# GNN layer on one core: layer 3's weights copied to SBUF by ScalarE, and the order of VectorE's step changed

## The reference, cut to what matters

```
h = relu(layernorm(x))                      # 12500 nodes x 128
l1 = per-node linear of h                   # 128 values: 32 scalars, 3 x 32 vectors
rbf = cut(d) * sin(n*pi*d/6) / (n*pi*d/6)   # 8 values for each of 200000 edges
weight = silu(silu(rbf @ fc_w1) @ fc_w2) @ fc_w3     # scales left out; 4 x 32 per edge
w00, w01, w10, w11 = split(weight, 4)
gs, gv = l1[src]                            # gather by edge
o00 = w00 * gs * sh0
o01 = w01 * gs * sh1                        # 3 x 32
o10 = w10 * gv * sh0                        # 3 x 32
o11 = w11 * sum_m(gv * sh1) / sqrt(3)
agg = segment_sum([o00, o11, o01, o10], dst) / count
out = x + sc(h) + tanh(agg @ alpha_w) * (agg @ lin2)
```

## Time and profile before

| | us |
|---|---|
| median of 3 runs (lowest, highest) | 2507.67 (2504.34, 2520.52) |
| the profiled execution | 2501.21 |
| its span, from first to last instruction | 2499.4 |
| first gather starts, last gather starts | 69.3, 2470.5 |
| mean granted clock of PE, share of full speed | 0.829 |

### The profile page before, as it was taken

How to read it: one execution, slowest core, us unless ns; L and a number is a source line. 1 busy time by engine, 2 the same in 40 slices (tenths; PEclk the granted TensorE clock), 3 DMA queues, 4 the chain that set the end, 5 groups by cost and what they waited for, 6 DMA issues and landing times. The chain is left out here.

```text
span 2499.4 us, 33478 instructions
## 1 busy us (share of the span) xinstructions
PE 1807.8 (72%) x7969; PEld 1166.1 (47%) x7969; DVE 1770.3 (71%) x4669; ACT 1018.1 (41%) x3049; POOL 1529.5 (61%) x1624
## 2 busy tenths in 40 slices
PE   6467667776887777777677776677776777877777
PEld 5244445444554444444444444444544544544444
DVE  7576677667667767766676667767676766677677
ACT  6344444444444444333333333334443433334343
POOL 7466566666666666666666666666565656556563
PEclk9688888888877888778787878889888888889879
DMA  7322222222222222222222222223232222222232
GB/s 213 67 63 66 53 66 66 59 62 66 64 56 65 65 58 62 55 49 51 46 51 48 48 48 52 58 45 67 53 67 55 63 63 64 53 64 59 60 66 55
DMA packets 347698, 155.72 MB, mean 62 GB/s; under 512 B 237983, under 2 KB 322048, under 8 KB 347584
## 3 DMA queue, kind: packets, MB, share of 16 engines
q0 software_dynamic: 50016, 102.51, 15.7%
q1 hardware_dynamic: 296938, 51.75, 11.4%
q10 hardware_dynamic: 630, 0.29, 0.0%
HBM read 134.27 MB, written 20.15 MB: 62 GB/s over the span
## 5 line engine op out<-in xcount | busy, mean ns | idle before, releaser
L967 POOL DMA_INDIRECT lin_g<-lin_table,src_ix x1563 | 1480.4, 947 | 929.4 <-issue 454.5
L1154 ACT ACTIVATE lin_sh<-lin_g,harm 128x128 f32<-128x128 f32 x1563 | 484.0, 394 | 256.3 <-DMA lin_g<-lin_table,src_ix 249.7
L1398 DVE TENSOR_TENSOR msg<-lin_sh,ps_w 128x576 f32<-128x576 f32 (+1 forms) x261 | 196.0, 751 | 520.1 <-remote 293.3
L1037 PE MATMUL ps_sums<-near_sums,far_hot 128*128 128x257 f32 x520 | 207.7, 487 | 433.8 <-DVE agg L1457 165.0
L1015 PE MATMUL ps_w<-w,h 128*128 128x256 f32 x1566 | 473.7, 448 | 61.6 <-DVE msg L1403 50.9
L1027 PE MATMUL ps_near<-msg,onehot 128*64 128x257 f32 x3126 | 500.3, 465 | 0.0
L1015 PEld LDWEIGHTS ps_w<-w,h 128*128 128x128 f32 x1566 | 400.8, 275 | 179.2 <-DVE msg L1403 63.7
L1161 ACT ACTIVATE near_sums<-ps_near 128x257 f32<-128x257 f32 x261 | 100.5, 385 | 809.5 <-remote 519.2
L996 PE MATMUL ps_h<-rbf,w 32*128 32x192 f32 x1044 | 271.4, 384 | 155.8 <-DVE rbf L1352 75.3
L1027 PEld LDWEIGHTS ps_near<-msg,onehot 128*64 128x64 f32 x3126 | 239.1, 162 | 226.0 <-issue 172.7
L1037 PEld LDWEIGHTS ps_sums<-near_sums,far_hot 128*128 128x128 f32 x520 | 102.7, 228 | 501.9 <-issue 356.8
(11 more groups left out here) (174 smaller groups left out, 1556.5 us busy)
## 6 DMA issues: line engine op xcount, KB each, us to landing
lin_g<-lin_table,src_ix POOLq DMA_INDIRECT x1563
dist_in<-in_edge_weight SPq DMA_DIRECT2D x67, 96.0 KB
lin_table<-lin_out SPq DMA_DIRECT2D x24, 256.0 KB, 2.4
x_in<-in_x SPq DMA_DIRECT2D x24, 256.0 KB
skip_table<-x_in SPq DMA_DIRECT2D x24, 256.0 KB
xq<-in_x SPq DMA_DIRECT2D x23, 256.0 KB, 3.6
harm<-in_edge_attr SPq DMA_DIRECT2D x66, 48.0 KB
x_in<-skip_table SPq DMA_DIRECT2D x8, 256.0 KB
```

What stands on the lines that cost most here:

```text
L967: pool.indirect_dma_start(slot_tiles(s, u)[rows, t, :], None, lin_table, bass.IndirectOffsetOnAxis(ap=src_ix[rows, s.phase, u, col:col + 1 ...
L1037: pe.matmul(ps_nodes(i), far_hot[:, u, :], near_sums[:, u % 2, :], start=True, stop=True).then_inc(sums_ready, 1)
L1154: last = act.activation(lin_sh0[:, u % 2, j, :], slot_tiles(s, u)[:, j, :], ACT.Copy, scale=harm[:, s.phase, u, harm_col(j):harm_col(j) + 1])
L1398: dve.tensor_tensor(o10[:, h], scaled[:, h, MUL:].rearrange("p t (m c) -> p t m c", m=3), spread_m(w_part(2))[:, h], ALU.mult)
```

## The change

Three edits. `copy_w(g+1)`, new, on ACT between `silu2` and `scale_lin`: one activation of 768 columns from `ps_w` to `w_sb`, two buffers in SBUF that share the memory of `key_all` (used only before the first group). It waits for `w_ready` of its group and for `w_read` of the group two before. PE's `layer3` now waits for `w_copied` in place of `w_read`, and `late` waits for `w_copied` in place of `w_ready` and reads the weights from `w_sb`. On DVE `products(g+2)` and `columns(g+2)` now stand ahead of `late(g+1)`, for which `dot` has two buffers. Before the first group ACT waits until all keys are stored, and copies group 0's weights ahead of the first two `scale_lin`.

```diff
+            w_sb = key_all
-            dot = s2("dot", [P, TILES, MUL])
+            dot = s2("dot", [P, 2, TILES, MUL])
...
-            def w_part(i):
-
-                return ps_w[:, 0:TILES * P].rearrange("p (t w c) -> p t w c", t=TILES, c=MUL)[:, :, i, :]
+            def w_part(u, i):
+
+                return w_sb[:, u % 2, :].rearrange("p (t w c) -> p t w c", t=TILES, c=MUL)[:, :, i, :]
...
-                            at_least(pe, w_read, i * SLOTS + u)
+                            at_least(pe, w_copied, i * SLOTS + u)
...
+                        def copy_w(i, u):
+
+                            i, u = i + u // SLOTS, u % SLOTS
+                            n = i * SLOTS + u
+                            act.wait_ge(w_ready, n + 1)
+                            at_least(act, w_read, n - 1)
+                            act.activation(w_sb[:, u % 2, :], ps_w[:, 0:TILES * P], ACT.Copy).then_inc(w_copied, 1)
...
+                        for b in range(GB):
+                            act.wait_ge(key_out[b], 16)
+                        copy_w(0, 0)
                         for u in range(2):
                             scale_lin(turn_of(0), u)
...
                                     silu2(i, u + 2)
+                                copy_w(i, u + 1)
                                 if share and u == 0:
                                     center(i)
...
-                            dve.wait_ge(w_ready, n + 1)
+                            if last_group(i):
+                                dve.wait_ge(msg_ready, n)
+                            dve.wait_ge(w_copied, n + 1)
                             dve.wait_ge(lin_sh0_ready, n + 1)
...
+                                if not last or u < SLOTS - 1:
+                                    products(s, u + 2)
+                                    columns(s, u + 2)
                                 late(s, u + 1)
                                 if u == 2 and share:
                                     skip_sum(i)
                                 if u == 2 and not last:
                                     fractions(i + 2)
-                                if not last or u < SLOTS - 1:
-                                    products(s, u + 2)
-                                    columns(s, u + 2)
```

More of the change, by code:

```diff
@@ L644, in gnn_kernel @@
             key_all = s2("key_all", [P, 2, GROUP])
+            w_sb = key_all
+            assert GB == 3
             harm = s2("harm", [P, RING, SLOTS, 4 * TILES])
@@ L722, in gnn_kernel @@
             h1_done, h1_ready, h2_done, h2_ready = sem("h1_done"), sem("h1_ready"), sem("h2_done"), sem("h2_ready")
-            w_ready, w_read, msg_ready, sums_ready = sem("w_ready"), sem("w_read"), sem("msg_ready"), sem("sums_ready")
+            w_ready, w_copied, w_read = sem("w_ready"), sem("w_copied"), sem("w_read")
+            msg_ready, sums_ready = sem("msg_ready"), sem("sums_ready")
             onehot_ready, lin_sh_ready, dot_ready = sem("onehot_ready"), sem("lin_sh_ready"), sem("dot_ready")
@@ L1385, in columns @@
                             dve.wait_ge(lin_sh_ready, n + 1)
-                            dve.tensor_reduce(dot[:, h], lin_sh[:, h].rearrange("p t m c -> p t c m"), AX_X, ALU.add).then_inc(dot_ready, 1)
+                            dve.tensor_reduce(dot[:, u % 2, h], lin_sh[:, h].rearrange("p t m c -> p t c m"), AX_X, ALU.add).then_inc(dot_ready, 1)
                         def late(s, u):
@@ L1394, in late @@
                             scaled = lin_sh0[:, u % 2]
-                            dve.wait_ge(w_ready, n + 1)
+                            if last_group(i):
+                                dve.wait_ge(msg_ready, n)
+                            dve.wait_ge(w_copied, n + 1)
                             dve.wait_ge(lin_sh0_ready, n + 1)
                             at_least(dve, near_ready, n - 1)
-                            dve.tensor_tensor(o10[:, h], scaled[:, h, MUL:].rearrange("p t (m c) -> p t m c", m=3), spread_m(w_part(2))[:, h],
+                            dve.tensor_tensor(o10[:, h], scaled[:, h, MUL:].rearrange("p t (m c) -> p t m c", m=3), spread_m(w_part(u, 2))[:, h],
                                               ALU.mult)
-                            dve.tensor_tensor(o00[:, h], scaled[:, h, 0:MUL], w_part(0)[:, h], ALU.mult)
-                            dve.tensor_tensor(w_s[:, h], w_part(1)[:, h], lin_s(s, u)[:, h], ALU.mult).then_inc(w_s_ready, 1)
+                            dve.tensor_tensor(o00[:, h], scaled[:, h, 0:MUL], w_part(u, 0)[:, h], ALU.mult)
+                            dve.tensor_tensor(w_s[:, h], w_part(u, 1)[:, h], lin_s(s, u)[:, h], ALU.mult).then_inc(w_s_ready, 1)
                             dve.wait_ge(dot_ready, n + 1)
-                            dve.scalar_tensor_tensor(out=o11[:, h], in0=dot[:, h], scalar=float(3 ** -0.5), in1=w_part(3)[:, h],
+                            dve.scalar_tensor_tensor(out=o11[:, h], in0=dot[:, u % 2, h], scalar=float(3 ** -0.5), in1=w_part(u, 3)[:, h],
                                                      op0=ALU.mult, op1=ALU.mult).then_inc(w_read, 1)
```

## The result

The changed kernel takes 2485.53 us (median of 4 runs, 2480.2 to 2493.36) where the kernel before, run beside it, takes 2509.92 us. The ratio is 0.990, 95% interval 0.9866 to 0.9935: 1% faster. The profiled execution took 2485.61 us, its span 2483.8 us, at a mean granted clock of 0.826.

A forecast was written before the change was run, and what follows sets the result against it. POOL's program, its gathers plus 475 us of stops, was taken as the span. The profiled 2501.2 + 14 - 12 + 1 = 2504 us, with the median 6.5 us above, gave 2510, own range 2485 to 2532, 8 in 10 2440 to 2580.

The forecast's parts named there:

- The step that failed: POOL's program is the span; only its 475 us of stops, or the 1.25 us per gather, can move the time much.
- the move: DVE's products and columns put ahead of the message: VectorE's waits shrink beside POOL's stops; cost 0, no gain.
- The other half of the step: PE's semaphore updates are late during a long run of POOL gathers and come about 2.5 us after it ends.
- Operands from SBUF: Four instructions of late, now with both operands in SBUF, delay POOL's gathers: 14 us, ends 0 and 70.
- the quadratic bound of 0.27 us a group: Upper end for gathers beside late: every gather beginning inside a two-SBUF-operand product waits for the rest; 70 us in all.
- 6 ns for each L1436: Small price of a DVE instruction with two SBUF operands, from mean gather times of 0.943 to 0.945 against 0.946 us.
- rival 2: Slower by the port: VectorE's SBUF operands lengthen POOL's gathers, up to 70 us, 2566 us; chance 0.2.
- Layer 3 freed from o11: PE's layer 3 waits for the copy and no longer for o11: a gain of 12 us, ends 0 and 53.
- The copy: ACT's 768-column copy from PSUM, 0.80 us each: cost 0 under the new order, 104 us without that cover.
- Rival 3: Slower by ACT: it stops at the copy for layer 3's late update, delaying scale_lin and copy_near; 104 us, 2612; chance 0.1.
- The start: Group 0's copy and a scale_lin delay its message up to 2.7 us, layer 3 starts 0.8 earlier: 1 us cost.
- Rival 1: Faster: the new order gets PE's updates out before they are held and POOL's stops go; 78 us, 2432; chance 0.27.

The follow-up runs named there:

- the order alone: Kernel before with only VectorE's new order (products and columns ahead of the message), no copy: 0.9798, 0.9857 and 0.9901 of the kernel before.
- set 4: Changed kernel (0.9921), the order alone (0.9901), the copy alone (1.0238), and changed kernel with layer 3 also waiting for w_read (0.9927); kernel before 2512.91 us.
- set 2: Kernel before, changed kernel, the order alone, and changed kernel with layer 3 also waiting for w_read, on one chip: 0.9996, 0.9972, 0.9857, 1.0025 of 2218.14 us.
- set 1: The order alone, the copy alone and the unread copy, beside the kernel before (2561.44 us) on one chip: 0.9798, 1.0066, 0.9852.
- set 3: The order alone plus one unused VectorE product per group, second operand in SBUF (0.985) or PSUM (0.9884); also the unread copy (0.9921) and a POOL memset (0.9971).
- the unread copy: Changed kernel, its copy made and waited for, but the message reads PSUM and layer 3 also waits for w_read: 0.9852 and 0.9921 of the kernel before.
- the copy alone: Kernel before with only ACT's copy, which the message reads and layer 3 waits for, VectorE's order as before: 1.0066 and 1.0238 of the kernel before.

## Why the prediction was wrong

**The step that failed** is the first: "POOL's program is the span, and only its 475 us of stops, or a change of the 1.25 us, can move the time by much." Busy and idle time of an engine always add up to the span; that shows which rows to count, not which engine limits. By it the move was put at 0, since VectorE's waits "lie beside POOL's stops and give nothing themselves"; the order alone gave 26 us (set 4), 31 us (set 2) and 52 us (set 1), which is why the kernel became faster where no change was foretold. Where updates are late, gathers made longer by 38 us (set 3, where only an operand's place differs) or 53 us (set 4) cost nothing that can be told from zero, and a double pause of POOL (388 us of memset) cost nothing, though it let updates out besides. POOL's stops took this up: they are slack there, not a fixed 475 us. What is left as the source of the period of some 9 us a group are the late updates that PE's partners wait for: DVE took 196 us more work at little or no loss, and on the chip with prompt updates the same program needs 290 us less. This is by exclusion and comparison, not followed link by link.

The other half of the step, the rule that updates come some 2.5 us after a run of gathers ends, is borne out by the profile of before. Of PE's five updates a group the trace holds 1091; 511 come more than 1 us behind the modelled end, and 391 of these come 1 to 3 us after the last gather ended, though POOL was more than 1 us past a gather for only 290 us of the span. On the chip of set 2 no update is that late, in runs of up to 50 gathers.

**Operands from SBUF**, +14 us, ends 0 and 70. As a length of gathers it was 3.5 times too small: +49.6 us here, 38 to 58 in the sets. The mechanism was right, a gather that starts within such a product waits, and the quadratic bound of 0.27 us a group was near the 0.22 us of set 2 (58.0/261). The rule of the Trainium skill (SBUF — State Buffer, section "Who interferes with whom"), that the second of the two blocks fully, came nearer than my row for the length of the gathers; for the time it would have been further off. The traces bear it out for one side alone: in set 2 the 187 first products of the message that began within a gather took 0.751 us, the others 0.754. The error was in preferring 6 ns for each L1436, from a difference of 1 ns between mean durations of two stretches, when such means differ by 2 ns from one another anyway. As a price in time it is 5 us or nothing on a chip with late updates (0.9921 against 0.9901, intervals overlapping), since the stops give it back; up to 25 us and more on the chip of set 2. So rival 2 had its cause (0.979 us a gather, the sign I gave was 0.98) without its effect.

**Layer 3 freed from o11**, a gain of 12 us, ends 0 and 53. Set 4 shows 0.0006 of the ratio, 1.5 us, within the interval; set 2 shows 12 us. The gain that I bounded at 53 us "where the rate is worse than the 8.96 us of the cycle" is there, 22 of it in just those stretches, less 6 in between; but by the sets it belongs to the order.

**The move**, cost 0, and nothing given. The order alone is 1.0 to 2.0% faster in three sets, and the whole of the gain: this the sets show. What I called lying "beside POOL's stops" was the place where time is made. The likely way is that with `products` and `columns` done while VectorE waits, only the message is left after a release; the chain from that to a shorter time isn't shown link by link.

**The copy**, cost 0. True only under the new order, where copy and operands together cost nothing that shows in set 4 and the unread copy costs 0.5% in set 1, and not true of the copy alone, 0.7 and 2.4%. I priced it at 104 us without cover; 57 were measured at most. Rival 3 was real, and the move of the block is its cure. ACT's copy took 0.818 us on average, 0.80 foretold.

**The start**, +1 us: the first message began 3.4 us earlier, 1.2 of it by an earlier first gather. Small, and wrong in sign.

**Rival 1**, stops that go because updates get out sooner, had 0.27. Stops did fall, but by the same 50 us by which the gathers grew; under 400 us, its sign, they were not. Its time was right in direction, and its 78 us too large. The sum of 2504 rested on two terms that hardly count on such a chip, and the gain came from the term that I had at zero. The 2485.5 us measured lie within the range for 8 in 10, and just inside the forecast's own range of 2485 to 2532, but 1% under the value.

The version that beats both kernels is the order alone: 0.9857 against 0.9972 on one chip, 0.9901 against 0.9921, not to be told apart, on the other.

## What to carry to other kernels

An engine whose busy and idle time fill the span isn't thereby the limit: put a known pause into it, and see whether the time moves (and whether the pause itself changes when others are released, as it did here). Before copying an operand out of PSUM, look at which instructions then have two operands in SBUF and what GpSimd does beside them; and move such work into a wait that is there already, since the same copy cost 2.4% in one order and nearly nothing in the other. Measure both versions on one chip.

## What was not expected of the hardware

- On four of the five sets' chips PE's semaphore updates were late, and on one they were prompt (0.02 us behind the modelled end, 2.4 us in the profile of before), with the same program, gathers of 0.944 to 0.947 us in both, and 2218 against 2509 to 2561 us. The forecast's rule that updates come some 2.5 us after a run of gathers ends holds in the one kind of chip, then, and not in the other. Where they were late, breaks in the runs helped (1.5 us of memset a group: 0.6% less time), letting POOL run freely hurt (7.3% more). Whether the matmuls or only their updates are late, and why one chip shows neither, wasn't found.
- The waiting goes one way: a gather within a product of two SBUF operands is held until about the product's end (0.28 us longer with 0.41 us left), while the product takes 0.750 us in that set's changed kernel and 0.748 in its kernel before.
